# Spreading the first group's routing weights inside the first layer's expert passes

## The chip, the cores and the metric

The kernel runs on one core of a Trainium2 chip. The metric is the device time of one execution in microseconds (us), lower is better. Engine names: TensorE (PE; its weight loads are PEld), VectorE (DVE), ScalarE (ACT), GpSimd (POOL), SyncE (SP, which only issues DMAs here).

## The reference

The input x has 4096 tokens (4 batches of 1024) of 128 elements. Two layers follow each other, each as expert block, attention, expert block ("macaron"), every block with a layer norm ahead of it and added to x:

```python
x = x + 0.5 * _L0_ffn_ref(_layernorm(x), ...)     # ffn0a
x = x + _L0_attn_ref(_layernorm(x), ...)          # 16 heads, causal softmax
x = x + 0.5 * _L0_ffn_ref(_layernorm(x), ...)     # ffn0b
x = x + 0.5 * _L1_ffn_ref(_layernorm(x), ...)     # ffn1a
x = x + _L1_attn_ref(_layernorm(x), ...)          # gated attention
x = x + 0.5 * _L1_ffn_ref(_layernorm(x), ...)     # ffn1b
```

The first layer's expert block routes each token to 4 of 16 experts of width 64 (sigmoid scores, a choice of 2 of 4 groups first) and adds a shared expert. It is computed densely: all experts are computed for all tokens, and `comb`, which is zero for experts not chosen, weights them:

```python
h = silu(einsum('td,eid->tei', xf, w1)) * einsum('td,eid->tei', xf, w3)
y = einsum('tei,edi,te->td', h, w2, comb)
z = silu(xf @ ws1.T) * (xf @ ws3.T) @ ws2.T
```

## The kernel before

The work is cut into stages, each a `Block` of the program: setup (`phase_setup`, L86), the expert pass ffn0a (`phase_moe`, L469), the attention (`phase_attention`, L849), ffn0b, and then the second layer's stages. In a stage every engine has its own list of instructions, and between two stages no engine goes on before all have arrived. Before TensorE's first instruction of a stage the trace shows this as a wait for PEq.

An expert pass works through 8 groups of 512 tokens (g0 to end). For each group and each chunk c of 128 inner columns (9 in the first layer: two experts in each of 8, the shared expert in the ninth), TensorE makes gate (L575) and up (L578) with three matmuls each (high and low parts of an fp32 split), ScalarE applies silu (L632), VectorE multiplies by the routing weights (`scale`, L695) and by up (`hide`, L705), ScalarE cuts the high part of the product (L637), GpSimd the low part (L665), and TensorE projects it down (L587 to L589), two chunks later. Gate and up have three PSUM buffers each, so that TensorE can be up to three chunks ahead of VectorE's product. Between these, `slot` spreads the next groups' work over the chunks: norm statistics (L371), routing (`r1` to `r5`), and the transposes.

The routing weights of a group arrive as a [16, 512] tile `combt`, one row for each expert. `scale` wants them as [128, 512]: rows 0 to 63 all expert 2c, rows 64 to 127 all expert 2c + 1. SyncE makes this in two steps, both in `sync` of `routing` (L253):

- `rows(g)` (L256) waits for `combt` and writes it to a scratch tensor in DRAM, `weight_rows` (two buffers, g % 2).
- `shares(g)` (L264) waits for that write, and then issues 16 DMAs, two for each of 8 slots e: each reads one row of 2 KB and spreads it over 64 partitions of `big[:, e, :]`. Ahead of each slot it calls `free(g, e)`, which waits until the slot is no longer read.

```python
def shares(g):
    sp.wait_ge(rows_out[g % 2], 16 * (g // 2 + 1))
    for e in range(r.SLOTS):
        free(g, e)
        for h in range(r.HALVES):
            ...
```

VectorE's `scale(g, c)` waits for the semaphore of its slot, `share_in[c]`, just before it reads it (L694).

Who issues `shares`: inside a pass, SyncE's list (L544) has for each g > g0 `rows(g)` and `shares(g)`. The first group's are issued by the stage ahead. For ffn0a that is the setup: SyncE's list ends with `rows` and `shares` of g0 (L118, L119). For ffn0b it is the attention: its order of work is made from a table of times (L926), in which the next pass's entries stand in `beside_attention`, `rows` at 0.81 and `shares` at 1.30 sections, the latter behind the last section's end. Its `free` (L1241) waits until the last attention product has been computed, because `big` holds the attention's probabilities until then. The attention's tail behind that (normalizing, output projection, addition to x at L1204) does not use `big`.

`phase_moe` also gets `ahead`: work for the stage behind. In ffn0a it is `Clearing`, whose loads are empty; in ffn0b `SplitAhead`, whose SyncE part loads the second layer's weights in pieces (L1365), two in the iteration of each group, from g0 on. A piece loaded in the iteration of g is split in the next group's part of the pass (L1374).

The second layer's passes get their first shares in other ways (`beside_pass` and `beside_gated`), and use the same `routing` and `phase_moe`.

Of the kernel before, what the change touches and what calls it, by code (L numbers as in the profile page):

```python
# [85 lines left out]
def phase_setup(nc, k, t, a, lead):  # L86
# [3 lines left out]
    with ExitStack() as ctx:  # L90
# [17 lines left out]
        @block.sync  # L108
        def _(sp):
            sp.dma_start(raw_rt[:], a["ffn0_router"]).then_inc(small_in, 16)  # L110
            for n in range(3):
                sp.dma_start(raw[:, n, :], a["ffn0_w"][:, n, :]).then_inc(w_in[n], 16)
            sp.dma_start(raw_att[:].rearrange("p w r -> p (w r)"), a["att_w"][:, 0:3 * P]).then_inc(att_in, 16)
            sp.dma_start(t.wo_t[:], a["att_w"][:, 3 * P:4 * P]).then_inc(att_in, 16)
            sp.dma_start(t.b_in[:], a["att_b"]).then_inc(att_in, 16)
            sp.dma_start(t.bo[:], a["L0_attn_b_out"].partition_broadcast(P)).then_inc(att_in, 16)
            later = lead.sync(sp, lambda g, e: None)
            later["rows"](lead.g0)  # L118
            later["shares"](lead.g0)  # L119

        @block.scalar
        def _(act):
# [78 lines left out]
def routing(nc, k, layer, turn_no, prior=None):  # L201


    first = layer == 0
    NE = E0 if first else E1
    ROUTE = 12 if first else 8
    r = Core()
# [5 lines left out]
    r.g0 = turn_no * NG  # L213
    r.end = r.g0 + NG
    r.w, r.router_in, r.router_count = k.w[layer], None, 0
    sems, own = k.moe_sems[layer], k.route_tiles[layer]

    def sem(name):
# [250 lines left out]
def phase_moe(nc, k, tag, r, follow, ahead=None, out=None):  # L469

    first, g0, end = r.first, r.g0, r.end
# [5 lines left out]
    SLOTS, PER, NSCALED, HALVES = r.SLOTS, r.PER, r.NSCALED, r.HALVES  # L477
# [20 lines left out]
    def follows(h, c, steps):  # L498

        if follow is not None:  # L500
            for back, at, name, n in follow.beside_pass:
                if (h, c) == (end - back, at) and name in steps:
                    steps[name](n)

    def piece_at(g, c):
        n = 2 * (g - g0 - 1) + (0 if c == PIECES[0] else 1)
        return n if ahead is not None and g > g0 and c in PIECES and n < ahead.count else None

    with ExitStack() as ctx:
        def sb(name, shape, dt=F32):  # L510
# [10 lines left out]
        gate_done, up_done, silu_done, scaled, hidden = (sem(s) for s in  # L521
            ("gate_done", "up_done", "silu_done", "scaled", "hidden"))
# [4 lines left out]
        @block.sync  # L527
        def _(sp):
            def used(g, e):
                sp.wait_ge(scaled, (g - 1) * NSCALED + (e + 1) * PER)  # L530

            def used_last(g, e):
                sp.wait_ge(scaled, (end - 1) * NSCALED + (e + 1) * PER)

            steps = r.sync(sp, used)
            if out is not None:
                stored = sem("stored")

            def store(g):
                sp.wait_ge(y_added, g + 1)  # L540
                sp.dma_start(out.rearrange("b (n p) d -> p (b n) d", p=P)[:, (g - g0) * TG:(g - g0 + 1) * TG, :],
                             k.x[:, rows(g)].rearrange("p (n d) -> p n d", d=D)).then_inc(stored, 16)

            for g in range(g0, end):  # L544
                if g > g0:
                    steps["rows"](g)
                    steps["shares"](g)
                elif ahead is not None:
                    ahead.load_plain(sp)
                if out is not None and g > g0:  # L550
                    store(g - 1)
                for c in range(NC):
                    if piece_at(g + 1, c) is not None:
                        ahead.load(sp, piece_at(g + 1, c))
            if out is not None:
                store(end - 1)
                sp.wait_ge(stored, 16 * NG)
            if ahead is not None:
                ahead.end(sp)
            if follow is not None:  # L560
                later = follow.sync(sp, used_last)
                for c in range(NC):
                    follows(end - 1, c, later)
# [285 lines left out]
def phase_attention(nc, k, own, a, begun, lead):  # L849
# [4 lines left out]
    SECTIONS = B * H // HG  # L854
    SCALE = float(np.float32(1.0 / np.sqrt(DH)))
    UNITS = [(qg, kb) for qg in range(HALF) for kb in range(TG * (qg + 1))]
    NU = len(UNITS)
# [7 lines left out]
    MAXB = (((3, 0),), ((4, 0),), ((5, 0),), ((6, 0),), ((7, 0),), ((0, 0), (2, 0)),  # L865
            ((7, 1),), ((4, 1), (6, 1)), ((1, 0), (5, 1)))
    HALF1 = next(i for i, parts in enumerate(MAXB) if any(c > 0 for _, c in parts))

    def width_of(t, c):
# [73 lines left out]
    with ExitStack() as ctx:  # L943
# [3 lines left out]
        def sem(name):  # L947
            return ctx.enter_context(nc.semaphore(f"att_{name}"))
# [26 lines left out]
        attended, o_copied = sem("attended"), sem("o_copied")  # L975
# [14 lines left out]
        def drained(eng, *entry):  # L990
            n = SLOT[entry]
            eng.wait_ge(emptied[n % RING], n // RING + 1)

        def unit_of(n, u):
            return n * NU + u

        def walk(parts, ahead):
            for kind, *at in ORDER:
                if kind in parts:
                    parts[kind](*at)  # L1000
                elif kind == "lead" and at[0] in ahead:
                    ahead[at[0]](at[1])
# [205 lines left out]
        @block.sync  # L1208
        def _(sp):
            def maxt(n):  # L1210
                drained(sp, "maxt", n)
                for part in range(2):
                    r = part * HG * NB
                    sp.dma_start(q_st[MROW + part * HG:MROW + (part + 1) * HG, n % 3, :].bitcast(F32), m_t[r:r + HG * NB, :])\
                      .then_inc(max_in, 16)

            def queries(n):
                b, hg = n // HG, n % HG
                for h in range(HALF):
                    drained(sp, "proj", b, 0, h)  # L1220
                sp.wait_ge(qk_again, 4 * b + 2)
                if n >= 3:
                    sp.wait_ge(scored, 2 * unit_of(n - 2, 0))
                sp.dma_start(q_st[0:MROW, n % 3, :].bitcast(F32), parts[hg * 32:hg * 32 + 32, 0, :, :].bitcast(F32))\
                  .then_inc(q_in[n % 3], 16)
                sp.dma_start(q_st[MROW:MROW + 2 * HG, n % 3, :].bitcast(F32),
                             k_pad[3 * DH:3 * DH + 2 * HG, 0, 0, :].bitcast(F32)).then_inc(q_in[n % 3], 16)

            def keys(n, h):
                b, hg = n // HG, n % HG  # L1230
                drained(sp, "proj", b, 1, h)
                if n >= 2:
                    sp.wait_ge(scored, 2 * unit_of(n - 2, (NU - TG, NU)[h]))
                cut = slice(h * G, (h + 1) * G)
                sp.wait_ge(qk_again, 4 * b + 3 + h)
                for j in range(HG):
                    rows = slice((hg * HG + j) * DH, (hg * HG + j) * DH + DH)
                    sp.dma_start(k_pad[3 * DH * j:3 * DH * (j + 1), n % 2, j, cut].bitcast(F32),
                                 parts[rows, 1, :, cut].bitcast(F32)).then_inc(k_in[n % 2][h], 16)

            def free(g, e):  # L1241
                sp.wait_ge(attended, SECTIONS * NU)

            walk(dict(maxt=maxt, queries=queries, keys=keys), lead.sync(sp, free))
            sp.wait_ge(max_in, 32 * SECTIONS)

        @block.vector
# [529 lines left out]
def build(nc, a, out):  # L1777
    k = Core()
    lay, npack = pack_layout()
    with ExitStack() as ctx:  # L1780
# [49 lines left out]
        k.w = [weights(0, lambda name, shape, dt: layer0.enter_context(nc.sbuf_tensor(f"{name}0", shape, dt))), None]  # L1830
        att = attention_tiles(lambda name, shape: early.enter_context(nc.sbuf_tensor(f"att_{name}", shape, F32)), arena)
        ffn0a = routing(nc, k, 0, 0)
        ffn0a.router_in, ffn0a.router_count = ctx.enter_context(nc.semaphore("router_in")), 1
        phase_setup(nc, k, att, a, ffn0a)

        def batch_ahead(stage, stack, beside_pass, unit, shift):
# [5 lines left out]
        phase_moe(nc, k, "ffn0a", ffn0a, begun, Clearing(nc, k, ctx, att))  # L1842

        ffn0b = routing(nc, k, 0, 1)
        ffn0b.routes = True
        g = ffn0b.g0
# [3 lines left out]
            (0.39, "rstd", g + 1), (0.42, "logit", g), (0.43, "lout", g), (0.46, "norm", g + 1), (0.48, "norm2", g + 1),  # L1850
            (0.50, "lturn", g), (0.51, "tanh", g), (0.53, "r1", g), (0.56, "r2", g), (0.60, "r3", g), (0.65, "r4", g),
            (0.70, "r5", g), (0.80, "cturn", g), (0.81, "rows", g), (0.90, "turn", g + 1), (0.91, "xh", g + 1),
            (0.92, "xl", g + 1), (1.30, "shares", g)]
        phase_attention(nc, k, att, a, begun, ffn0b)
        early.close()

# [7 lines left out]
        for n, (high, low) in enumerate(((w1.wgh, w1.wgl), (w1.wuh, w1.wul), (w1.wdh, w1.wdl))):  # L1864
            for c in range(0, C1 * P, AHEAD):
                cut = slice(c, min(c + AHEAD, C1 * P))
                pieces.append((a["ffn1_w"][:, n, cut], high[:, cut], low[:, cut]))
        ffn1a = routing(nc, k, 1, 0, prior=ffn0b)
        ffn1a.routes, ffn1a.router_in, ffn1a.router_count = True, sems.split, 1
        g = ffn1a.g0  # L1870
# [7 lines left out]
        with ExitStack() as own:  # L1878
            ahead = SplitAhead(nc, own, sems, "w1", pieces, (), ())
# [6 lines left out]
        with ExitStack() as own:  # L1886
            zeros = ((gau.ones[:].bitcast(F32), 1.0),)
            ahead = SplitAhead(nc, own, sems, "gau", gau.pieces, gau.plain, zeros, base=len(pieces))
# [3 lines left out]
        g = ffn1b.g0  # L1892
# [75 lines left out]
```

## Time and profile before

| what | us |
|---|---|
| median of 3 runs | 1777.79 |
| lowest and highest of them | 1774.81, 1777.92 |
| the profiled execution: its time | 1778.24 |
| its span, first to last instruction | 1776.5 |
| setup, to the first matmul of ffn0a | 36.4 |
| ffn0a, to the first matmul of the attention | 192.2 |
| attention, to the first matmul of ffn0b | 616.1 |

The mean granted clock of TensorE over the span is 0.974 of the full one. Times in rows are microseconds from the span's start unless marked ns. In a timeline a row gives start, duration, engine, line, operation, output and input, and, in brackets, how long the engine had been idle and what ended it. A "q" behind an engine is its instruction queue: issues, waits and borders. Several instructions that follow each other are merged into one row (x16), whose duration runs from the first start to the last end.

### The profile page before, as it was taken

The page shows a single profiled execution, that of the slowest core. Times are in us where ns is not written, and L with a number is a line of the kernel's source. Part 1 is how long each engine was busy: PE and PEld are TensorE (multiplying, and loading weights), DVE is VectorE, ACT ScalarE, POOL GpSimd, SP SyncE. Part 2 cuts the span into 40 slices and gives each one's busy share as a digit, 9 for nine tenths or more (in the row PEclk, how much of TensorE's full clock was granted, in tenths as well). Part 3 has the DMA queues.
Part 4 walks back from the last instruction along what each step waited for, and adds up shares of the span by engine and source line. Part 5 has one row for each costly group of instructions (what it writes and reads, how often), then busy time and mean ns, then how long its engine had stood idle before and what let it go on. Part 6 is the DMA issues. An engine that isn't in the chain of part 4 may idle for free. (4 is left out here: it accounts for less than half of the span.)

```text
span 1776.5 us, 25917 instructions
## 1 busy us (share of the span) xinstructions
PE 1634.1 (92%) x8360; PEld 1160.4 (65%) x8360; DVE 1287.4 (72%) x3879; ACT 1017.1 (57%) x1718; POOL 776.3 (44%) x734
## 2 busy tenths in 40 slices
PE   3999879899999989997999999999998988999998
PEld 2777645555556555554777767777777876777776
DVE  4777658788778878872777767777765876767775
ACT  3666415565566566665666646555555645555554
POOL 1566611311311312112566646555574625555555
PEclk9999958999999999998999999999999998999999
DMA  4222211111111112101233332111110002111120
GB/s 149 76 87 88 91 33 24 21 30 24 23 32 22 25 20 35 20 11 42 75 121 120 103 100 83 54 49 48 49 48 1 1 1 90 60 55 60 55 94 20
DMA packets 58246, 95.01 MB, mean 53 GB/s; under 512 B 9312, under 2 KB 17120, under 8 KB 58112
## 3 DMA queue, kind: packets, MB, share of 16 engines
q1 hardware_dynamic: 56000, 91.07, 18.1%
q10 hardware_dynamic: 2112, 2.30, 0.4%
q8 instruction: 66, 1.08, 0.3%
q14 instruction: 68, 0.56, 0.1%
HBM read 76.76 MB, written 2.88 MB: 45 GB/s over the span
## 5 line engine op out<-in xcount | busy, mean ns | idle before, releaser
L695 DVE TENSOR_TENSOR big<-banks,big 128x512 f32<-128x512 f32 x384 | 264.7, 689 | 211.5 <-ACT banks L632 175.5
L1157 ACT ACTIVATE big<-banks 128x1024 f32<-128x1024 f32 (+3 forms) x384 | 301.8, 811 | 172.9 <-PE banks L1068 167.0
L632 ACT ACTIVATE banks<-banks 128x512 f32<-128x512 f32 x384 | 223.9, 583 | 275.9 <-PE banks L575 270.6
L705 DVE TENSOR_TENSOR big<-big,banks 128x512 f32<-128x512 f32 x400 | 274.9, 687 | 29.8 <-PE banks L578 15.8
L1049 PE MATMUL banks<-arena 128*128 128x512 f32 (+3 forms) x768 | 250.1, 402 | 27.1 <-DVE att_mx L1285 15.4
L1197 POOL TENSOR_SCALAR_AFFINE_SELECT big<-big 128x512 f32<-128x512 f32 x128 | 81.6, 637 | 401.9 <-ACT big L1157 401.9
L1285 DVE CUSTOM_DVE_ANT_0 banks<-banks,att_mask 128x128 f32<-128x128 f32 (+3 forms) x512 | 234.0, 525 | 28.9 <-PE banks L1049 28.2
L665 POOL TENSOR_TENSOR ffn1b_hid_l<-big,ffn1b_hid_h 128x512 fp32r<-128x512 f32 x128 | 165.6, 1294 | 128.6 <-ACT ffn1b_hid_h L637 128.6
L1068 PE MATMUL banks<-arena 128*128 128x512 f32 (+3 forms) x768 | 206.3, 354 | 12.1 <-ACT big L1157 12.0
L665 POOL TENSOR_TENSOR ffn1a_hid_l<-big,ffn1a_hid_h 128x512 fp32r<-128x512 f32 x128 | 165.5, 1293 | 118.3 <-ACT ffn1a_hid_h L637 118.3
L575 PE MATMUL banks<-xh,arena 128*128 128x512 f32 x512 | 208.9, 408 | 8.3 <-PEq L1451 6.9
L1049 PEld LDWEIGHTS banks<-arena 128*128 128x128 f32 x768 | 134.4, 197 | 116.1 <-DVE att_mx L1285 49.2
L578 PE MATMUL banks<-xh,arena 128*128 128x512 f32 x512 | 203.7, 398 | 0.0
L1287 DVE TENSOR_REDUCE att_mx<-banks 128x1 f32<-128x512 f32 x256 | 161.1, 683 | 26.5 <-PE banks L1049 25.9
L1068 PEld LDWEIGHTS banks<-arena 128*128 128x128 f32 x768 | 133.1, 190 | 41.1 <-ACT big L1157 26.3
L1087 PE MATMUL banks<-big,att_v_aug 128*32 128x512 f32 (+3 forms) x1536 | 144.8, 494 | 0.6 <-POOL big L1197 0.6
L665 POOL TENSOR_TENSOR ffn0a_hid_l<-big,ffn0a_hid_h 128x512 fp32r<-128x512 f32 x72 | 92.8, 1289 | 84.9 <-ACT ffn0a_hid_h L637 84.9
L665 POOL TENSOR_TENSOR ffn0b_hid_l<-big,ffn0b_hid_h 128x512 fp32r<-128x512 f32 x72 | 93.2, 1294 | 62.1 <-ACT ffn0b_hid_h L637 61.6
L575 PEld LDWEIGHTS banks<-xh,arena 128*128 128x128 f32 x512 | 97.3, 190 | 29.6 <-issue 9.0
L578 PEld LDWEIGHTS banks<-xh,arena 128*128 128x128 f32 x512 | 97.3, 190 | 22.3
L578 PE MATMUL banks<-xl,arena 128*128 128x512 f32 x256 | 102.0, 399 | 0.0
L575 PE MATMUL banks<-xl,arena 128*128 128x512 f32 x256 | 101.2, 395 | 0.0
(256 smaller groups left out, 3175.8 us busy)
## 6 DMA issues: line engine op xcount, KB each, us to landing
big<-weight_rows SPq DMA_DIRECT2D x256, 128.0 KB, 2.9
big<-weight_rows SPq DMA_DIRECT2D x128, 256.0 KB, 4.2
arena<-att_parts SPq DMA_DIRECT2D x16, 384.0 KB
arena<-att_parts SPq DMA_DIRECT2D x128, 48.0 KB
w_raw<-in_ffn_w_dram SPq DMA_DIRECT2D x12, 256.0 KB, 2.9
out_dram<-x SPq DMA_DIRECT2D x8, 256.0 KB, 2.3
setup_raw<-in_ffn_w_dram SPq DMA_DIRECT2D x3, 576.0 KB, 7.2
gau_angle<-in_consts_dram SPq DMA_DIRECT2D x2, 512.0 KB, 7.2
```

Source lines behind the costliest of these rows:

```text
L575: mm = pe.matmul(gate_ps[:, num % NB, :], w[:, ws], xx[:, g % 2, :], start=m == 0, stop=m == 2)
L578: mm = pe.matmul(up_ps[:, num % NB, :], w[:, ws], xx[:, g % 2, :], start=m == 0, stop=m == 2)
L632: act.activation(gate if c < NSCALED else sil, gate, ACT.Silu).then_inc(silu_done, 1)
L665: pool.tensor_tensor(hid_l[:, num % NH, :], hid[:, num % NH, :], hid_h[:, num % NH, :].bitcast(F32), ALU.subtract).then_inc(low_cut, 1)
L695: dve.tensor_tensor(scl[:, num % 2, :], gate_ps[:, num % NB, :], share[:, c // PER, :], ALU.mult)\
L705: dve.tensor_tensor(hid[:, num % NH, :], scl[:, num % 2, :] if c < NSCALED else sil, up_ps[:, num % NB, :], ALU.mult).then_inc(hidden, 1)
L1049: mm = pe.matmul(bank[:, at:at + width], q_st[:, n % 3, t * P:(t + 1) * P], k_pad[:, n % 2, j, c * G:c * G + width], start=True, stop=True ...
L1068: mm = pe.matmul(score_ps[:, pair, h, 0:c], k_pad[:, n % 2, 2 * pair + h, kb * P:(kb + 1) * P], q_st[:, n % 3, (qg + 1) * G - c:(qg + 1) * ...
L1087: mm = pe.matmul(o_ps[32 * j:32 * j + 32, G - c:G], v_aug[:, b % 2, kb, at:at + 32], probs[:, unit % NPROB, j, 0:c], start=kb == 0, stop=k ...
L1157: act.activation(probs[:, unit % NPROB, 2 * pair:2 * pair + 2, 0:c], score_ps[:, pair, :, 0:c], ACT.Exp, scale=SCALE).then_inc(exped, 1)
L1285: ins = dve.tensor_tensor_reduce(now, now, mask[:, G - width:G], 1.0, -3e38, ALU.add, ALU.max, best)
L1287: ins = dve.tensor_reduce(best, now, AX.X, ALU.max)
```

## The change

`shares` of the first group leaves the setup's and the attention's SyncE lists and becomes the first thing in SyncE's list of the pass itself, for the first layer's two passes (`spread_late` is true for them alone). `rows` stays where it was. Inside the pass, `used` no longer waits for the first group, since nothing in the pass has read a slot before it. With `shares` gone from the attention's order, its `free` is replaced by one that does nothing. The second layer's passes issue what they issued before.

```diff
@@ phase_setup, block.sync
             later = lead.sync(sp, lambda g, e: None)
             later["rows"](lead.g0)
-            later["shares"](lead.g0)
@@ routing
     r.w, r.router_in, r.router_count = k.w[layer], None, 0
+    r.spread_late = first
@@ phase_moe, block.sync
             def used(g, e):
-                sp.wait_ge(scaled, (g - 1) * NSCALED + (e + 1) * PER)
+                if g > g0:
+                    sp.wait_ge(scaled, (g - 1) * NSCALED + (e + 1) * PER)
...
             for g in range(g0, end):
                 if g > g0:
                     steps["rows"](g)
+                if g > g0 or r.spread_late:
                     steps["shares"](g)
-                elif ahead is not None:
+                if g == g0 and ahead is not None:
                     ahead.load_plain(sp)
@@ phase_attention, block.sync
-            def free(g, e):
-                sp.wait_ge(attended, SECTIONS * NU)
-
-            walk(dict(maxt=maxt, queries=queries, keys=keys), lead.sync(sp, free))
+            walk(dict(maxt=maxt, queries=queries, keys=keys), lead.sync(sp, lambda g, e: None))
             sp.wait_ge(max_in, 32 * SECTIONS)
@@ build, ffn0b.beside_attention
-            (0.92, "xl", g + 1), (1.30, "shares", g)]
+            (0.92, "xl", g + 1)]
```

## Rows read from the trace of the kernel before

**Rows 1.** The page, part 1, engine TensorE: busy time, share of the span, instructions.
```profile
PE 1634.1 (92%) x8360; PEld 1160.4 (65%) x8360; DVE 1287.4 (72%) x3879; ACT 1017.1 (57%) x1718; POOL 776.3 (44%) x734
```

**Rows 2.** Timeline of SyncE alone: start us, us, engine, line, operation, tiles, count.
```profile
24.03 0.34 SPq L256 DMA_DIRECT2D weight_rows<-combt  x1
25.63 10.11 SPq L264 DMA_DIRECT2D big<-weight_rows  x16
...
56.57 0.32 SPq L256 DMA_DIRECT2D weight_rows<-combt  x1
58.15 10.03 SPq L264 DMA_DIRECT2D big<-weight_rows  x16
...
833.60 10.09 SPq L264 DMA_DIRECT2D big<-weight_rows  x16
```

**Rows 3.** Timeline of all engines at the end of the setup stage.
```profile
25.91 0.69 DVE L390 TENSOR_TENSOR xl<-banks,xh 128x512 fp32r<-128x512 f32 x1 [3.01 <-ACT xh L327]
26.51 0.22 DVE L198 COPY att_mask<-pack 128x128 f32<-128x128 f32 x1
...
36.42 0.76 PE L575 MATMUL banks<-xh,wgh 128*128 128x512 f32 x1 [11.18 <-PEq L90]
```

**Rows 4.** Timeline at the end of the attention stage.
```profile
843.08 1.26 POOL L1204 TENSOR_TENSOR x<-x,att_ypos 128x512 f32<-128x512 f32 x1 [1.34 <-DVE att_ypos L1326]
...
844.66 0.36 SPq L1365 DMA_DIRECT2D w_raw<-in_ffn_router_dram  x1
...
844.69 0.76 PE L575 MATMUL banks<-xh,wgh 128*128 128x512 f32 x1 [5.32 <-PEq L943]
```

**Rows 5.** Timeline at the border between first pass and attention.
```profile
227.60 0.69 DVE L687 SCALAR_TENSOR_TENSOR x<-banks,x 128x512 f32<-128x512 f32 x1 [7.17 <-PE banks L605]
228.61 1.94 PE L1013 MATMUL banks<-pack,att_xn 128*128 128x128 f32 x8 [1.05 <-PEq L509]
```

**Rows 6.** Timeline of the first pass behind group 0's, VectorE's first scaling.
```profile
61.68 0.69 DVE L695 TENSOR_TENSOR big<-banks,big 128x512 f32<-128x512 f32 x1 [1.86 <-DMA big<-weight_rows]
```

**Rows 7.** The instructions on weight_rows, 27 to 36 us: duration, starts; landing.
```profile
L264 SPq DMA_DIRECT2D big<-weight_rows x14: 596/597/603, 26.8 to 35.1; - x14
...
DMA to landing us min/median/max: 2.8/2.9/3.4
```

**Rows 8.** First pass: two scalings in the timeline, then TensorE's waits, 35 to 60 us.
```profile
38.69 0.69 DVE L695 TENSOR_TENSOR big<-banks,big 128x512 f32<-128x512 f32 x1 [11.96 <-ACT banks L632]
...
40.82 0.67 DVE L695 TENSOR_TENSOR big<-banks,big 128x512 f32<-128x512 f32 x1
...
PEld banks L587 <- POOL ffn0a_hid_l L665: 1.8, 5, 0.6
```

**Rows 9.** Timeline of the second pass's first chunks.
```profile
846.96 0.69 DVE L695 TENSOR_TENSOR big<-banks,big 128x512 f32<-128x512 f32 x1 [3.96 <-ACT banks L632]
...
848.29 0.86 DVE L371 BATCH_NORM_STATS2 st<-x 128x6 f32<-128x128 f32 x4
...
848.73 0.58 ACT L632 ACTIVATE banks<-banks 128x512 f32<-128x512 f32 x1 [1.80 <-PE banks L575]
...
849.34 0.69 DVE L695 TENSOR_TENSOR big<-banks,big 128x512 f32<-128x512 f32 x1 [0.18 <-ACT banks L632]
```

**Rows 10.** The instructions on w_raw, 840 to 900 us, ScalarE's alone.
```profile
L1374 ACT ACTIVATE arena<-w_raw x2: 299/462/624, 876.9 to 884.5; 128x128 fp32r<-128x128 f32 x1, 128x512 fp32r<-128x512 f32 x1
```

**Rows 11.** Stretches: length, busy time by engine, granted clock, DMA share, GB/s.
```profile
250.00:260.00 10.00, 10.00 (x22) 5.53 (x21) 10.00 (x25) 0.00 (x0) 0.00 (x0) 0.50 0.12 19
...
847.00:848.20 1.20, 1.20 (x4) 0.95 (x3) 1.17 (x2) 0.00 (x0) 0.00 (x0) 0.50 0.21 79
848.20:852.00 3.80, 3.80 (x17) 2.88 (x16) 3.44 (x15) 2.83 (x5) 1.89 (x2) 0.98 0.00 0
...
1470.50:1473.00 2.50, 2.50 (x6) 2.02 (x7) 0.23 (x1) 0.58 (x1) 0.00 (x0) 0.50 1.02 365
1473.00:1476.00 3.00, 3.00 (x9) 2.22 (x9) 1.82 (x3) 1.12 (x2) 0.09 (x1) 0.50 0.15 57
```

## The prediction

> **What bounds the kernel now.** Start with the page's busy times. TensorE is busy for 92% of the span [rows 1], so a change of a few instructions on SyncE can only matter where TensorE stands still. Next read SyncE alone in order of time [rows 2]. The sixteen DMAs that spread a group's weights take 10.1 us to issue, wherever they stand, and for the very first group they stand at the end of the setup stage, from 25.63 to 35.74 us. Then read all engines around that place [rows 3]: VectorE's last instruction of the setup ends at 26.73 (26.51 + 0.22), and the first matmul of the expert pass starts at 36.42, after 11.18 us of idle time. In between this view has instructions of SyncE alone. The border between two stages lets no engine through until every engine has arrived, so here SyncE's issuing, and nothing that is computed, sets the start of the first pass.
>
> The other place that the change touches is the end of the attention stage. There the same sixteen issues run from 833.60 to 843.69 [rows 2], but GpSimd's last addition starts at 843.08 and lasts 1.26 us, to 844.34, and the pass starts at 844.66 to 844.69 [rows 4]. SyncE is done first. At this border the issuing is covered, by 0.65 us.
>
> **What is removed.** (1) Setup, sixteen issues at its end. SyncE's last issue in the setup is then the rows DMA, at 24.03 and 0.34 us long [rows 2], and VectorE arrives last, at 26.73. What does a border cost after VectorE? Two estimates. At the next border VectorE ends last too, at 228.29 (227.60 + 0.69), and the first matmul starts at 228.61 [rows 5]: 0.32 us. At the present one SyncE's last issue ends at 35.74 and the matmul comes at 36.42: 0.68 us. I take 0.32, since there the same engine is last; the other end costs 0.36 more. The first matmul moves from 36.42 to 27.05: **9.37 us earlier** (9.0 at the other end).
>
> (2) Attention, sixteen issues at its end. GpSimd ends last without them as well: **0**. Below zero there is at most the 0.32 us by which GpSimd's end precedes the start, if its recorded end is rough. The removed wait on the attended counter was passed while the tail still had work, and nobody waits for SyncE there.
>
> **What is added.** The same sixteen issues stand at the head of SyncE's list in both passes. SyncE leaves the border together with TensorE (844.66 against 844.69 [rows 4]). Slot 0 needs two DMAs. The price from the first issue to the multiplication that waited for it can be read directly: in the pass behind the first one, issues begin at 58.15 [rows 2] and VectorE, idle on this DMA for 1.86 us, starts at 61.68 [rows 6]: 3.53 us. The landing times agree: 2.8 to 3.4 us, median 2.9, behind a second issue that starts 0.6 later [rows 7]. The wait for the rows DMA ahead of them costs nothing: SyncE got past it at 25.63 in the old trace, before the new border.
>
> (3) First pass. The first scaling now starts at 38.69, 2.27 us behind the first matmul [rows 3, 8]; it will start 3.50 us behind it. **+1.23 us**, if all of it reaches TensorE. Does it? VectorE's list is in order: scaling, product, statistics, scaling of chunk 1 at 40.82, without a gap. TensorE's projections wait for what follows from it: 1.8 us in five waits on GpSimd's low part in this pass, with none longer than 0.6 [rows 8]. So TensorE has no reserve at chunk 1, and I take all of it. The lower end is 0.6: ScalarE's and GpSimd's instructions stand between VectorE and the projection, and if their own lists hold them back, that reserve is at most of the size of these waits. The upper end is 1.7, with a landing of 3.4 instead of 2.9.
>
> (4) Second pass. The first scaling is at 846.96, again 2.27 us behind the first matmul. Here VectorE has a little reserve: its statistics end at 849.15 (848.29 + 0.86), and it then waits until 849.34 for ScalarE's activation, which ends at 849.31 [rows 9]. 1.23 - 0.19 gives **+1.04 us** (0.4 to 1.5). The instructions behind are those of the first pass, so the delay arrives at TensorE in the same way.
>
> (5) The other slots. Their DMAs follow 0.64 us apart (26.8 to 35.1 in 13 steps [rows 7]), 1.27 per slot, while VectorE takes a new chunk after 2.13 us (38.69 to 40.82 [rows 8]). Slot 1 lands at 4.8 us, and it is wanted at 5.6 (3.50 plus 2.13); each later one has more reserve: **0**. If cover is gone, that is if a slot took more than 2.1 us, the seven slots behind it would each add the excess.
>
> (6) What is queued behind the issues. In the first pass SyncE has nothing before the rows of group 1, at 56.57 [rows 2]. The issues end at 27.05 + 10.1 = 37.2. In the second pass the two loads for the next layer's weights move from 844.66 to about 854.8; their first use is at 876.9 [rows 10]; with a landing of some 3 us the reserve is 19 us. **0** for both.
>
> **Sum.** -9.37 + 1.23 + 1.04 = **-7.10 us**. The profiled execution has 1778.24 us around a span of 1776.5, so it would become 1771.1. The median of the three runs shown is 1777.79, 0.45 lower, with 1774.81 as the lowest; 7.1 off the median is 1770.7. I say 1770.8.
>
> **Two rules against the rows.** The rule that speaks against this change: the Trainium skill, DMA: Bandwidth & Descriptors, Rules for kernel authors, advises to issue a DMA early, compute, and wait for it late, so that its fixed cost is covered. By that alone both early issues are covered, the change only adds its two stalls, +2.3, and the time would be 1780.1. The trace agrees for the attention, where the cover exists ([rows 4], and it makes the +1.04); in the setup the early issue is covered by nothing [rows 3], so that the rule's price there is only the 1.23.
>
> The clock is the second. The second pass begins at the lower level (granted clock 0.50, so 1.2 GHz) and is at the upper one from 848.20, 3.5 us behind its start; the last stage's pass has 0.50 still at 1473 to 1476, up to 5.5 us behind its start at 1470.50 [rows 11]. Were it 5.5 in the new first pass too, 2.0 us more at half rate would leave 1.0 us of work undone; but TensorE would be waiting for what follows from slot 0 during most of this, so I add nothing to the sum, and 1.0 to the upper end. The Trainium skill, TensorE: Matmul & The Clock Gate, Part 1, says that the number of matmuls that run slow at a start varies between executions of one kernel. No two executions are traced here that could show it.
>
> **Rivals.**
> (A) My forecast, 1770.8: 0.78.
> (B) The stalls are larger than one landing. The clock rises late (+1.0), landings are at 3.4 (+1.0 for both passes), and the border costs 0.68 (+0.36): -7.1 + 2.4 = -4.7, so 1773.1. For it: all three ends are in the rows. Against: they must fall together. If slots fall behind as well (0.3 us each for seven slots, +2.1), it is 1775.2, within 0.2%. 0.14, a third of it above 1774.2.
> (C) The change does not do what it says for the start: something other than SyncE holds the first border, such as a transfer that is still under way. Then only +2.3 remains: 1780.1, which is within 0.2%. Against: the first matmul follows SyncE's last issue by 0.68 us, though share transfers of 2.9 us were still in flight. 0.04.
> (D) Slower: the clock in the attention's first section. It stands at 0.50 from 250 to 260, with both TensorE and VectorE recorded as busy for all 10 us [rows 11]. If VectorE sets the pace there, the low level is free; an attention that starts 8 us earlier may meet the rise elsewhere. If the low level lasts into the part where TensorE sets the pace, each microsecond costs half of one. It decides from 14 us on, where the gain of 7.1 is used up, and is slower by over 0.2% from 21 us on; 25 us would give 1777.8 + 12.5 - 7.1 = 1783.2. Nothing excludes it but that such a stretch has never lasted. 0.04, and slower by over 0.2% in three quarters of it.
>
> **Numbers.** 0.2% of this kernel is 3.6 us, about what a measurement of it can tell from no change: the bounds are 1774.2 and 1781.4. Faster: 0.78 + two thirds of 0.14 = 0.87. Within: the third of (B), (C) and the rest of (D), 0.10. Slower: 0.03. The range: from 1770.8, the low ends of both stalls (-1.3), the 0.3 of (2) and a median most of the way to where the lowest run before lay (-2) give 1767.2; (B) gives 1773.1, and some of its upper part belongs in it too. I take 1767.2 to 1774.4.
>
> **What would show it.** In SyncE's list the rows DMA at 24.03 is followed by share issues from about 27.0 on, and those of the second pass begin with it, at 836.5 (844.69 less 8.14). The first matmul is at 27.05, and its idle time before it falls from 11.2 to about 1.8 us. VectorE's first scaling is released by the share DMA in both passes, 3.5 us behind the start, and no later scaling of these groups is. The attention starts 8.1 us earlier, at 220.5 instead of 228.61; the stage behind the second pass 7.1 us earlier. Wrong would be: a first matmul later than 28, a share wait on slots 1 to 7 in these groups, or stages after them that are longer than before.

## The result, and the profile after

| | before | changed |
|---|---|---|
| median of 6 runs each, us | 1775.9 | 1767.27 |
| lowest and highest | 1772.14, 1777.92 | 1764.2, 1770.8 |
| span of the profiled execution | 1776.5 | 1767.8 |
| ratio, with its 95% interval | | 0.9948 (0.9932 to 0.9965) |

The change makes the kernel faster: 0.9948 of 1775.9 is 9.2 us less, with an interval of 6.2 to 12.1. A second comparison (below) gave 0.9961 (0.9944 to 0.9979), 6.9 us. The forecast was 7.1 us and a time of 1770.8. The direction and the place of the gain were right, and the size is inside both intervals, but the time came out 3.5 lower. Of that, 1.9 is the base: with three more runs of the kernel before, its median is 1775.9 instead of 1777.79. The other 1.6 is in terms of the sum: above all, the price of the two stalls behind slot 0 was taken too high. The experiments show by how much.

SyncE's list after, start and duration in us, answers to [rows 2]:

```profile
23.70 0.34 SPq L256 DMA_DIRECT2D weight_rows<-combt  x1
26.66 10.10 SPq L264 DMA_DIRECT2D big<-weight_rows  x16
48.14 0.32 SPq L256 DMA_DIRECT2D weight_rows<-combt  x1
49.73 10.05 SPq L264 DMA_DIRECT2D big<-weight_rows  x16
...
817.20 0.33 SPq L256 DMA_DIRECT2D weight_rows<-combt  x1
835.78 10.08 SPq L264 DMA_DIRECT2D big<-weight_rows  x16
845.91 0.59 SPq L1364 DMA_DIRECT2D w_raw<-in_ffn_router_dram  x1
```

The sixteen issues take what they took, 10.1 us, but now they start together with the pass. The timeline of all engines after, at the end of the setup and in the first pass, answers to [rows 3, 8]:

```profile
26.17 0.21 DVE L197 COPY att_mask<-pack 128x128 f32<-128x128 f32 x1
26.66 10.10 SPq L264 DMA_DIRECT2D big<-weight_rows  x16
26.66 1.28 ACT L634 ACT_TABLE_LOAD   x1 [1.13 <-PEq L90]
26.70 0.76 PE L577 MATMUL banks<-xh,wgh 128*128 128x512 f32 x1 [1.79 <-PEq L90]
...
30.51 0.69 DVE L697 TENSOR_TENSOR big<-banks,big 128x512 f32<-128x512 f32 x1 [4.12 <-DMA big<-weight_rows]
...
32.62 0.67 DVE L697 TENSOR_TENSOR big<-banks,big 128x512 f32<-128x512 f32 x1
```

VectorE's last instruction ends at 26.38, and the first matmul follows 0.32 us behind it, at 26.70 instead of 36.42. The idle time before it is 1.79 us instead of 11.18. The new wait is the one on slot 0: VectorE starts 3.81 us behind the first matmul instead of 2.27. The scaling of the next chunk waits for no DMA.

How much of this stall reaches TensorE? Here is the first matmul of group 1, in the kernel before and in the changed one:

```profile
58.21 0.48 PE L575 MATMUL banks<-xh,wgh 128*128 128x512 f32 x1
49.77 0.48 PE L577 MATMUL banks<-xh,wgh 128*128 128x512 f32 x1
```

It comes 21.79 us behind the pass's first matmul (58.21 - 36.42), and after the change 23.07 us (49.77 - 26.70). In these two executions 1.28 us have arrived.

The end of the attention after, with the start of the second pass, answers to [rows 4, 9]:

```profile
834.21 1.26 POOL L1206 TENSOR_TENSOR x<-x,att_ypos 128x512 f32<-128x512 f32 x1 [1.34 <-DVE att_ypos L1325]
835.78 10.08 SPq L264 DMA_DIRECT2D big<-weight_rows  x16
835.78 1.28 ACT L634 ACT_TABLE_LOAD   x1 [7.19 <-PEq L945]
835.82 0.76 PE L577 MATMUL banks<-xh,wgh 128*128 128x512 f32 x1 [5.32 <-PEq L945]
...
839.32 0.69 DVE L697 TENSOR_TENSOR big<-banks,big 128x512 f32<-128x512 f32 x1 [5.19 <-DMA big<-weight_rows]
```

GpSimd still ends last, its last addition starts 1.61 us ahead of the first matmul as before (843.08 and 844.69), and TensorE's idle time of 5.32 us is the old one. The scaling of slot 0 starts 3.50 us behind the first matmul.

The two profiled executions, border by border: the start of the first pass is 9.72 us earlier, the first pass is 0.02 longer, the attention 0.83, the second pass 0.74, and all that follows is 0.57 shorter. That makes 8.70 us, the difference of the spans.

### The profile page after: what moved, and what is told of

It reads as the page before. It is cut to its first block and busy times, and to the rows that moved or that the text cites. A ratio compares the mean times of both kernels' runs of the same rounds, so it can differ in the third digit from the quotient of the medians.

```text
span 1767.8 us, 25916 instructions
## 1 busy us (share of the span) xinstructions
PE 1632.6 (92%) x8360; PEld 1159.7 (66%) x8360; DVE 1287.2 (73%) x3879; ACT 1016.6 (58%) x1718; POOL 775.2 (44%) x734
## 5 line engine op out<-in xcount | busy, mean ns | idle before, releaser
L577 PEld LDWEIGHTS banks<-xh,arena 128*128 128x128 f32 x512 | 96.9, 189 | 29.4 <-issue 8.9
```

Of the source, the lines that this page charges most:

```text
L577: mm = pe.matmul(gate_ps[:, num % NB, :], w[:, ws], xx[:, g % 2, :], start=m == 0, stop=m == 2)
```

## The experiments

Each table row that follows is one traced execution. A stage's length runs from its first matmul to the next stage's. "Slot 0" is the start of VectorE's first scaling behind the stage's first matmul.

| kernel | first matmul | first pass: slot 0, length | second pass: slot 0, length | attention |
|---|---|---|---|---|
| before | 36.42 | 2.27, 192.19 | 2.27, 189.30 | 616.08 |
| before, again | 36.45 | 2.27, 192.01 | 2.27, 191.27 | 616.62 |
| second pass only | 36.80 | 2.27, 191.59 | 3.47, 191.23 | 617.51 |
| slot 0 ahead | 27.55 | 2.27, 191.72 | 2.27, 190.85 | 615.18 |
| first pass only | 26.57 | 3.73, 192.15 | 2.27, 189.89 | 615.05 |
| changed | 26.70 | 3.81, 192.21 | 3.50, 190.04 | 616.91 |
| changed, again | 26.84 | 3.52, 193.19 | 3.48, 191.86 | 614.82 |
| slot 0 third | 26.79 | 5.95, 195.05 | 6.28, 194.56 | 615.88 |
| slot 0 last | 26.72 | 12.35, 202.19 | 12.87, 202.33 | 614.30 |

**1. One half of the change at a time.** From the changed kernel, the attention's half undone:

```diff
-    r.spread_late = first
+    r.spread_late = first and turn_no == 0
@@ phase_attention, block.sync
+            def free(g, e):
+                sp.wait_ge(attended, SECTIONS * NU)
+            walk(dict(maxt=maxt, queries=queries, keys=keys), lead.sync(sp, free))
@@ beside_attention
-            (0.92, "xl", g + 1)]
+            (0.92, "xl", g + 1), (1.30, "shares", g)]
```

> Only the first pass issues its first group's shares itself; the attention issues the second pass's as before. Theory P (each slot-0 stall passes through to the end): the changed kernel less its second stall of about 1.0 us, so about 8.4 us under the kernel before by the forecast's terms, and the second pass as long as before, 189.3 us. Theory Q (a stage gives a stall of about 1.2 us back before it ends): the same time as the changed kernel. Both: first matmul of the first pass at 26.7 to 27.1.

Measured: 1768.62 against 1777.95, ratio 0.9944 (0.9932 to 0.9955), 10.0 us less (8.0 to 12.1). This half holds the whole gain. Theory P's 8.4 lies in the interval too, so the time alone doesn't separate P from Q. The first matmul, at 26.57, is 0.13 earlier than the expected range.

The other half (`turn_no == 1`, and `shares` back in the setup):

> Only the second pass issues its first group's shares itself; the setup keeps its sixteen issues. Theory P: 1.0 us slower than the kernel before, the second pass 190.3 instead of 189.3 us long. Theory Q: no change, 189.3. A third possibility, that the attention was held up by the issues at its end: faster, the attention shorter than 616.1 us.

Measured: 1778.72 against 1777.95, ratio 1.0003 (0.9992 to 1.0013). Moving the issues away from the attention's end brings no gain that shows: the interval goes from 1.4 us less to 2.3 us more, and the attention, at 617.51 us, is not shorter. The loss of 1.0 us that P expected lies in that interval, as does Q's zero, so the time decides nothing between them. The traced second pass has 191.23 where P had 190.3; the table shows that two executions of the same kernel before have 189.30 and 191.27, so the length of one traced stage can't show a microsecond.

**2. Slot 0 ahead, the rest in the pass.** From the first-pass-only kernel (`shares` also gets the slots as an argument, here and in the next experiment):

```diff
@@ phase_setup
             later["rows"](lead.g0)
+            later["shares"](lead.g0, range(1))
@@ phase_moe, block.sync
-                    steps["shares"](g)
+                    steps["shares"](g, range(1, SLOTS) if g == g0 else range(SLOTS))
```

> As the first run here, but the two DMAs of slot 0 are issued at the end of the setup, and only slots 1 to 7 in the pass; the attention as before. Slot 0 then lands at about 28.5 to 28.9, before the first scaling wants it at 2.27 us behind the first matmul (29.0). Theory P: 1.2 us less than the first run here, less up to 0.4 us by which the border now comes later behind SyncE's last issue: first pass again 192.2 - 0, the DMA wait at the first scaling gone. Theory Q: not faster than the first run here.

Measured: 1769.99 against 1777.95, ratio 0.9944 (0.9928 to 0.996), the same ratio as the first-pass-only run. Its timeline, with SyncE's two issues of the setup first:

```profile
25.71 1.15 SPq L265 DMA_DIRECT2D big<-weight_rows  x2
26.59 0.22 DVE L198 COPY att_mask<-pack 128x128 f32<-128x128 f32 x1
27.51 1.28 ACT L635 ACT_TABLE_LOAD   x1 [1.56 <-PEq L90]
27.55 0.77 PE L578 MATMUL banks<-xh,wgh 128*128 128x512 f32 x1 [2.23 <-PEq L90]
...
29.82 0.69 DVE L698 TENSOR_TENSOR big<-banks,big 128x512 f32<-128x512 f32 x1 [3.01 <-ACT banks L635]
```

The wait is gone: the first scaling is 2.27 us behind the first matmul and is released by ScalarE. But the border costs more. SyncE's second issue ends at 26.86, just behind VectorE's end at 26.81, so SyncE arrives last again, and the first matmul follows it by 0.69 us, as it follows SyncE by 0.68 us in the kernel before, and not by the 0.32 us that it takes behind VectorE. The pass is only 0.4 shorter than in the first-pass-only run (191.72 against 192.15). In these two traces the dearer border (0.74 us from VectorE's end instead of some 0.3) takes up the gain, and the times show no difference either.

**3. Does a stall pass through?** Two doses. In the changed kernel, for the first group of both passes, the slots in another order, first 7 to 0, then 1, 2, 0, 3 to 7:

```diff
-                    steps["shares"](g)
+                    steps["shares"](g, range(SLOTS - 1, -1, -1) if g == g0 else range(SLOTS))
```

> As the changed kernel, but the eight slots of the first group are issued in the order 7 to 0 in both passes. Slot 0 lands 14 issues of 0.63 us later, so the first scaling comes at about 12.3 us behind the first matmul instead of 3.8: 8.9 us more stall in each pass. Theory P: 17.8 us slower than the changed kernel, about 1785. Theory Q: clearly less than that, each of the two stages under 8.9 us longer; if a stage can give back a fixed amount of 1 to 1.5 us, 15 us.

> As the changed kernel, but the first group's slots are issued in the order 1, 2, 0, 3 to 7 in both passes: slot 0 lands four issues, 2.5 us, later, so the first scaling comes 6.2 us behind the first matmul. Theory P (a stall passes through): each pass 2.5 us longer than the changed kernel's, 194.7 and 192.5 to 193.7, 5 us in all. Theory Q' (a stage gives back some 0.6 us and no more, as the stall of 10.1 us in the run with slot 0 last suggests): the same, 2.5 per pass. Theory Q (a stage gives small stalls back): each pass less than 1.5 us longer.

Measured: slot 0 last 1789.55 against 1777.95, ratio 1.0073 (1.0057 to 1.0089), 11.6 us over the kernel before in the medians. The changed kernel was 8.0 under it in the medians of its second comparison, so that makes some 19.6 us over the changed one, above P's 17.8. Slot 0 third 1775.88 against 1778.3, ratio 0.9987 (0.9975 to 0.9999); the changed kernel had 1770.27 beside the same runs of the kernel before, so 5.6 us more. TensorE in the run with slot 0 last, second pass, and below it the granted clock (the column behind the five engines) of two stretches there:

```profile
843.21 0.77 PE L577 MATMUL banks<-xh,wgh 128*128 128x512 f32 x1 [5.26 <-PEq L945]
...
856.08 0.69 DVE L697 TENSOR_TENSOR big<-banks,big 128x512 f32<-128x512 f32 x1 [14.56 <-DMA big<-weight_rows]
...
859.66 0.77 PE L589 MATMUL banks<-ffn0b_hid_h,wdh 128*128 128x512 f32 x1 [8.92 <-POOL ffn0b_hid_l L667]
```

```profile
843.00:856.00 13.00, 7.52 (x21) 5.66 (x21) 0.00 (x0) 2.45 (x3) 0.00 (x0) 0.76 0.57 183
856.00:860.00 4.00, 0.34 (x1) 0.38 (x2) 3.81 (x14) 1.98 (x4) 1.27 (x1) 0.50 0.03 12
```

TensorE runs ahead by its three buffers, then stands for 8.92 us until the low part of chunk 0 is there. In that time its clock falls from the upper level, 2.4 GHz, to the lower, 1.2, and behind the stand its matmuls start 0.43 us apart instead of 0.23 until 865.3. The first pass of this run has the same, until 46.1. So this run's passes hold a second price, that of the clock. In the run with slot 0 third TensorE's longest wait is 3.1 us in the second pass, followed by slow matmuls from 849.2 to 851.5, and 1.7 us in the first pass, with no slow matmuls behind it.

With the table: against the mean of the four first passes without a late slot 0 (191.88), a scaling late by 10.1 us costs 10.3, one late by 3.7 costs 3.2, and one late by 1.4 (mean of three) costs 0.6 (192.52). In the second pass, against 190.33: late by 10.6 costs 12.0, by 4.0 costs 4.2, by 1.2 costs 0.7 (mean of three, 191.04). So theory Q, that small stalls are given back, falls: for the 2.3 us more that the slot order 1, 2, 0 makes in the first pass over the changed kernel's stall, 2.5 arrive, and for 2.8 in the second pass 3.5, the fall of the clock included. P doesn't hold to the letter either: of the changed kernel's own stalls only a part is found.

The ends of the passes are a blunt place to see that part, since equal passes differ by 0.6 to 2.0 us there. The start of group 1, nine chunks in, is sharper. Its first matmul, in us behind the pass's first, one value for each trace:

| pass | slot 0 not late | late by 1.2 to 1.5 | slot 0 third | slot 0 last |
|---|---|---|---|---|
| first | 21.79, 21.99, 22.39, 22.34 | 23.24, 23.07, 22.79 | 25.19 | 32.26 |
| second | 22.08, 22.15, 22.27, 22.27 | 23.01, 22.79, 22.98 | 26.08 | 33.80 |

There no late value lies among the others, in either pass. In the means a stall of 1.42 us has cost TensorE 0.91 in the first pass, and one of 1.21 has cost 0.73 in the second: some 0.5 us of each is taken up before group 1. With slot 0 third, 3.06 of 3.68 arrive in the first pass, where the clock stays up: again 0.6 less, in one trace. That is what Q' says, for stalls up to 3.7 us. In the second pass 3.89 of 4.01 arrive, and with slot 0 last 10.13 of 10.08 and 11.61 of 10.60. These three come with the fall of the clock, so they can't say whether the same half microsecond is in them.

Where does that reserve come from? TensorE's timeline in the run with slot 0 ahead, where no share is late:

```profile
31.10 0.63 PE L578 MATMUL banks<-xh,wgl 128*128 128x512 f32 x1
31.53 0.63 PE L581 MATMUL banks<-xh,wuh 128*128 128x512 f32 x1
31.95 0.63 PE L581 MATMUL banks<-xl,wuh 128*128 128x512 f32 x1
32.38 0.63 PE L581 MATMUL banks<-xh,wul 128*128 128x512 f32 x1
32.81 0.57 PE L288 MATMUL banks<-xh,rth 128*128 128x512 f32 x1
33.21 0.40 PE L289 MATMUL banks<-xl,rth 128*128 128x512 f32 x1
33.45 0.39 PE L290 MATMUL banks<-xh,rtl 128*128 128x512 f32 x1
```

The starts are 0.43 us apart up to 32.81, then 0.23: in this execution TensorE is slow for 5.7 us behind its start. How long it is slow varies between executions of the same first pass: 3.1 and 3.5 us in the two traces of the kernel before, 5.7 in the second-pass-only run, whose first pass is that of the kernel before, 3.9 and 4.4 in the changed kernel, and 6.0 in the first-pass-only run. A late clock and a late slot 0 run beside each other. Where TensorE is slow for 5.7 us and no share is late, GpSimd's first low part ends at 6.7 us and the first projection starts at 7.5 to 7.6, so TensorE has 0.8 us in hand. In the first-pass-only run, with slot 0 late by 1.5, the low part ends at 7.2, only 0.5 later, and the first projection starts at 7.6 all the same. There the stall costs the first projection nothing. In the first trace of the kernel before, low part and projection are at 6.2 and 6.3; in that of the changed one both are at 7.3, and TensorE waits 0.4 us. So a late clock can hide a stall at the first projection. It isn't the whole account: the first-pass-only run still starts group 1 some 0.9 us later than the two with the same slow start (23.24 against 22.39 and 22.34). Where the rest of the half microsecond is taken up was not tested.

**4. The same kernels again.** To see how steady the stages are:

> The changed kernel once more, for a second trace and more times. If its stages are steady: first matmul at 26.6 to 26.7, first pass 192.2, second pass 190.0 to 191.2, 8 to 10 us under the kernel before. If the first weight load's landing (0.3 to 0.4 us earlier in the three kernels without share DMAs in the setup than in the three with them) is chance, its activation starts anywhere from 6.5 to 7.4; if it belongs to the change, at 6.6 to 6.7.

> The kernel before once more, for a second trace. If its stages are steady: first matmul at 36.4 to 36.8, first pass 191.6 to 192.2, second pass 189.3 to 190.8. If the early landing belongs to the change, the first weight's activation starts at 7.0 to 7.4 here.

Measured: changed 1770.27 against 1778.3, ratio 0.9961 (0.9944 to 0.9979); the kernel before once, 1779.96. The stages are less steady than expected. The changed kernel's first matmul came at 26.84 instead of 26.6 to 26.7, its first pass was 193.19, one microsecond longer than the first time, and its second pass 191.86, above 191.2; the kernel before's second pass was 191.27, above 190.8. The expectation of 6.6 to 6.7 for the first weight's activation was missed: it starts at 6.82. Its starts are 7.01, 7.04, 7.09, 7.35 and 7.40 in the five traces whose setup holds share DMAs (before, twice; slot 0 ahead; the last run below; second pass only), and 6.57 to 6.90 in the six where it holds none. From there to the first matmul the four traces with sixteen issues need 29.4 us, and the changed kernel's two 20.0.

**5. A version that beats both.** The waits in the later passes pointed to another place. In the first-pass-only run, from 50 us to near the end of the pass (waiting engine and line, what it waited for, us in total, times, longest):

```profile
PEld banks L589 <- POOL ffn0a_hid_l L667: 17.7, 39, 2.3
DVE big L697 <- DMA big<-weight_rows: 12.5, 6, 3.5
PE banks L589 <- POOL ffn0a_hid_l L667: 9.4, 16, 1.8
```

Every later group also begins with a wait for slot 0, because its weights are transposed only at chunk 7 of 9. One number, on top of the first-pass-only kernel:

```diff
-  ... r4=4, r5=5, cturn=7, yout=2, ...
+  ... r4=4, r5=5, cturn=6, yout=2, ...
```

> Only the first pass late, as in the first run here, and in the first layer's passes the transpose of the routing weights stands at chunk 6 instead of 7, so that each next group's shares are issued one chunk (2.2 us) earlier. In each later pass VectorE waits 1.6 to 3.9 us for slot 0. If these waits hold TensorE up: up to 1 us less in each of 14 passes, 5 to 14 us faster than the first run here. If the earlier transpose makes TensorE wait for VectorE's addition of the group ahead (about 0.9 us in each of 12 passes) as much as it gains: no change, or slower by up to 10 us.

Measured: 1761.58 against 1778.3, ratio 0.9907 (0.9892 to 0.9922), 16.5 us less than the kernel before. The same waits, 50 us to near the end of the pass:

```profile
PEld banks L589 <- POOL ffn0a_hid_l L667: 13.5, 33, 2.2
PEld banks L304 <- DVE comb L460: 6.0, 6, 1.0
PE banks L589 <- POOL ffn0a_hid_l L667: 3.5, 5, 1.8
DVE big L697 <- DMA big<-weight_rows: 2.9, 3, 1.5
```

The waits for the slots fall from 12.5 to 2.9 us, and TensorE's own for the low part from 9.4 to 3.5. The price is the new line for L304, the wait of TensorE's weight loads for the routing. The passes are 187.46 and 186.07 us long instead of 192.15 and 189.89, so both parts of the expectation happened, and the gain was the larger. Against the first-pass-only run, in medians of two comparisons, it is 7.0 us. Is it separate from the change? The same number alone, in the kernel before:

> The kernel before with the transpose of the routing weights at chunk 6 instead of 7 in the first layer's passes, and nothing of the change. If the gain of the run before (some 7 us over the first-pass-only run) comes from the later passes' waits for slot 0 and has nothing to do with the change: first and second pass at 187 and 186 us less the first pass's stall of 0.6, the time 7 to 10 us under the kernel before. If it needs the late issue in the first pass: no gain.

Measured: 1768.59 against 1777.89, ratio 0.9948 (0.9928 to 0.9967), 9.2 us less, with passes of 186.70 and 185.70 us. It needs nothing of the change, and within the intervals the two add up: 9.2 here, and 6.9 to 10.0 for the late issue, against 16.5 for both.

## Why the prediction was right, and where it failed

- **Step (1), setup, -9.37: right, and short by 0.4.** From the start of the first weight's activation to the first matmul, the old order needs 29.41 us (36.42 - 7.01) and the new one 20.01 (26.70 - 6.69): -9.40. The border behind VectorE cost 0.32, the value taken. Not in the sum was that the activation itself starts 0.43 us earlier on average (6.74 over six traces against 7.18 over five). No value of one group lies within the other. What makes the load land earlier stays open. Experiment 2 bears out both of the prediction's border prices, 0.32 behind VectorE and 0.68 behind SyncE.
- **Step (2), attention, 0: right.** Its length is 615.05 to 616.95 in the six traces with the issues at its end (the two of experiment 5 are among them, with 616.94 and 616.95), and 614.30 to 617.51 in the five without. The means are 616.1 and 615.9.
- **Step (3), first pass, +1.23: mis-sized, and this is the step that failed.** The stall itself was larger than taken: VectorE's first scaling starts 3.81, 3.73 and 3.52 us behind the first matmul, where 3.50 was forecast, so it is late by 1.42 us in the mean. But only 0.91 of that has reached TensorE at group 1, and 0.64 at the pass's end (192.52 - 191.88). What failed is "TensorE has no reserve at chunk 1, and I take all of it". The waits it was read from, 1.8 us in five, are those of the weight loads (PEld). The matmuls waited for GpSimd's low part once from 35 to 60 us in the kernel before:

```profile
PE banks L587 <- POOL ffn0a_hid_l L665: 0.2, 1, 0.2
```

  It was also read from one execution, whose clock had risen early; others are late at the first projection without any late share. In the pair of traces compared first, the stall did arrive, 1.28 us at group 1, and at the pass's end the difference was 0.02: that is chance as far as can be told, for the runs with a slow start and no late share were behind by 0.6 at group 1 too, and 0.5 to 0.6 ahead at the end.
- **Step (4), second pass, +1.04: mis-sized in the same way.** A stall of 1.21 us cost TensorE 0.73 at group 1. At the end the means differ by 0.7 too, but equal kernels differ by 2.0 there, so the end alone would show nothing. The reserve was some 0.5 us and not 0.19.
- **Step (5), the other slots, 0: right.** In the changed trace VectorE waits once for a share DMA before 50 us, 4.12 us for slot 0; later waits are those of the later groups, which the kernel before has too. **Step (6)**: right, the weight loads moved to 845.91 and nothing waited for them there.
- **The sum.** -9.40 - 0.43 + 0.6 + 0.7 = -8.5 us, against medians that differ by 8.6 and 8.0. The forecast of -7.1 was 1.4 short: 1.0 from the two stalls, 0.4 from the setup. That this sum meets the medians to 0.1 is luck, since its small terms are means of three or four traces that differ by up to 2 us. By the values at group 1 the stalls cost 0.9 and 0.7, and the sum is -8.2.
- **The two rules.** The rule on early issue, from the Trainium skill, DMA: Bandwidth & Descriptors, would alone have given a loss. It holds where there is work to cover the issue: at the attention's end, moving it gained nothing. In the setup the early issue was the cost. That the number of slow matmuls at a start varies (the Trainium skill, TensorE: Matmul & The Clock Gate, Part 1) could not be checked before. The traces agree: 3.1 and 3.5 us in the kernel before, and 5.7 in the same first pass of the second-pass-only run. The prediction put a late rise at the upper end of the range, as a cost; in the first-pass-only run it worked the other way, by hiding the stall from the first projection.
- **The rivals.** (B) came in part and did not cost what it said: the stall at VectorE was up to 0.3 us larger in the first pass, and the clock rose as late as 6.0 us behind the start, but what reached TensorE was less than forecast, and the border cost 0.32. (C) is excluded by the first matmul at 26.70. (D), the attention's clock, did not show, by the lengths of step (2). What follows did not become longer: from the second pass's end to the last instruction it is 742.5 and 741.9 us in the kernel before, 741.9 and 741.7 in the changed one.

## What to carry to other kernels

A queue that only issues DMAs can hold a whole stage back, if the stage's border waits for it. Look at who arrives last at each border, and price the issues there (0.6 us each in this kernel) and not by the landing of the data. Put the issues behind the border if nothing covers them, and leave them where something does. A stall that is read from one trace can hide behind another delay of the same start, so a term of one microsecond needs several traces, and it is seen more sharply soon behind its cause than at the end of a long stage. Waits of weight loads are not waits of matmuls: ask for the latter before you say that TensorE has no reserve. And after such a change, read the waits of the steady passes too: here a number in the order of work was worth as much as the change.

## What the runs showed of the hardware that was not expected

- In all traces the first pass's matmuls start 0.43 us apart for 3.1 us at least, over 6 in some. That is the lower level: in the second pass of the kernel before they stand 0.43 us apart where the column reads 0.50. But the granted clock of the first pass's slow stretch reads 1.00, as in the run with slot 0 ahead:

```profile
27.50:30.20 2.70, 2.65 (x6) 2.16 (x7) 0.38 (x1) 1.86 (x2) 0.00 (x0) 1.00 0.52 163
30.20:33.00 2.80, 2.80 (x8) 2.18 (x7) 2.40 (x7) 1.12 (x2) 0.04 (x1) 1.00 0.73 204
```

  So for the start of this program the spacing of the matmuls decides, not that column.
- A border costs more when SyncE arrives last with DMA issues than when a computing engine does: 0.68 us behind its last issue in the kernel before, with sixteen of them, and 0.69 with two (slot 0 ahead), against 0.32 behind VectorE.
- The first weight load landed some 0.4 us earlier in the kernels whose setup holds no share DMAs, although these come 20 us behind it.
